# Router logits as eight more columns of the value and output projections, and a new order of TensorE's and VectorE's work in a turn

## What is computed

```python
h = concat([patches(x) @ W.T + b + pos_embed, with a class token, txt])   # 32 x 274 x 192
h = h + attention(layernorm(h))        # 12 heads of 16, rotary positions, causal, then @ Wo + bo
n = layernorm(h)                       # (h - mean) / sqrt(var + eps), no gain
pc, pu = softmax(n @ Wsc + bsc), softmax(n @ Wsu + bsu)       # 4 logits each
common = expert[argmax pc](n)          # gelu(n @ W1 + b1) @ W2 + b2
unique = expert[argmax pu](n) for tokens beyond the capacity of their common expert
out = h + common + dropped * unique
```

## Time and profile before

| | us |
|---|---|
| median of 3 runs | 1303.76 (1300.44 to 1304.24) |
| the profiled execution | 1305.39, span 1303.5 |
| PE busy in the span | 1202.0 (92%), 12718 instructions |
| DVE busy | 883.1 (68%) |
| POOL, ACT busy | 621.8 (48%), 555.9 (43%) |
| granted TensorE clock, mean | 0.962 of full |
| ACT's exponential L760, 96 of 1631 ns | 156.6 |

### The profile page before, as it was taken

One profiled execution on the slowest core, in us unless ns is written; L12 is line 12 of the kernel. 1 busy time (PEld: TensorE's weight loads), 2 busy tenths in 40 slices (PEclk: granted clock), 3 DMA queues, 4 the chain that ended last, 5 costly groups with the idle time before them and its releaser, 6 DMA issues.

```text
span 1303.5 us, 33182 instructions
## 1 busy us (share of the span) xinstructions
PE 1202.0 (92%) x12718; PEld 1026.7 (79%) x12718; DVE 883.1 (68%) x1979; ACT 555.9 (43%) x959; POOL 621.8 (48%) x990
## 2 busy tenths in 40 slices
...
DMA packets 84367, 168.03 MB, mean 129 GB/s; under 512 B 16446, under 2 KB 57701, under 8 KB 84208
## 3 DMA queue, kind: packets, MB, share of 16 engines
...
...
## 4 chain that ended last, share of the span: by engine, by line
PE 46%; DVE 22%; issue 12%; POOL 12%; DMA 3%; ACT 2%; SPq 1%; POOLq 0%; DVEq 0%; ACTq 0%
PE h_ps L1677 10%; PE y_ps L1688 9%; DVE capped L995 4%; POOL sorted_d L235 4%; PE round_banks L591 3%; PE gen L553 3%; PE gen L511 3%; POOL PT L877 3%; DVE xn L1011 3%; PE round_banks L564 3%; PE gen L520 2%; DVE nm L999 2%; DVE nm L997 2%; POOL rstd L870 2%; PE round_banks L578 2%
## 5 line engine op out<-in xcount | busy, mean ns | idle before, releaser
L760 ACT ACTIVATE PT<-round_banks 128x1752 f32<-128x1752 f32 x96 | 156.6, 1631 | 175.4 <-PE round_banks L591 175.4
L877 POOL TENSOR_SCALAR_AFFINE_SELECT PT<-PT 128x512 f32<-128x512 f32 x192 | 117.8, 637 | 206.3 <-ACT PT L760 205.8
L1767 ACT ACTIVATE Gl<-h_ps,W 128x256 f32<-128x256 f32 x264 | 115.8, 474 | 172.1 <-PE h_ps L1677 163.9
L1688 PE MATMUL y_ps<-W,Gl 128*128 128x192 f32 x1056 | 181.2, 325 | 0.0
L1688 PEld LDWEIGHTS y_ps<-W,Gl 128*128 128x128 f32 x1056 | 171.3, 189 | 0.0
L1677 PE MATMUL h_ps<-XH,Wh 128*128 128x256 f32 x528 | 149.0, 299 | 7.0 <-DVE Wl L1834 2.8
L511 PE MATMUL gen<-w_emb,xT 128*128 128x192 f32 (+1 forms) x768 | 143.8, 339 | 7.8 <-DMA ident<-in_ident_dram 7.8
L1677 PE MATMUL h_ps<-XH,Wl 128*128 128x256 f32 x528 | 141.4, 289 | 0.0
L511 PEld LDWEIGHTS gen<-w_emb,xT 128*128 128x128 f32 (+1 forms) x768 | 119.6, 171 | 16.7 <-DMA ident<-in_ident_dram 7.8
L591 PEld LDWEIGHTS round_banks<-QKT 32*128 32x128 f32 x2304 | 95.3, 187 | 46.7 <-DVE nm L997 23.0
L995 DVE TENSOR_TENSOR capped<-round_banks,masks_f 128x1024 f32<-128x1024 f32 x96 | 116.2, 1211 | 17.3 <-PE round_banks L564 16.8
...
...
## 6 DMA issues: line engine op xcount, KB each, us to landing
...
```

Source lines behind the costliest of these rows:

```text
L760: act.activation(PT[(JG * b + j) % 2][:], R[:, :, 0:438], ACT.Exp, scale=SCALE).then_inc(exps, 1)
L877: pool.affine_select(x[:, :, at:at + P], x[:, :, at:at + P], [[0, GH], [1, P]], ALU.is_ge, 0.0, base=0, channel_multiplier=-1)
L1688: mm = pe.matmul(y_ps[t.par][:, k * D:(k + 1) * D], Gl[t.par][:, f, k * P:(k + 1) * P], W[t.i][:, W2O + f * D:W2O + (f + 1) * D], start=(f ...
L1767: act.activation(Gl[t.par][:, f, :], h_ps[f % 3][:, 0:ROWS], ACT.Gelu, bias=W[t.i][:, B1O + f:B1O + f + 1]).then_inc(g_ready, 1)
```

## The change

**Logits without the second transposes.** The normed token is (h - mean) / std, and h is the residual plus attention. The router weights are centred over their 192 rows (`centre_router`), so that the mean drops out. Then `n @ Wr = (h @ Wc) / std`, and h splits in two. The part of the residual is `xn @ Wc` times the first norm's std, with `xn` already turned for the projections: V0, V1 and Vt get eight more columns of `w_qkv`. The part of attention is `att @ (Wo @ Wc)`: WO and WOt get eight more columns of `w_o`, which are mixed once, in turns 1 and 2, on PE and DVE (`turn_output_weights`, `mix_output_weights`). ACT scales the first part by std into `part` while it copies the values (a second small activation behind each); POOL makes std (`spread`); DVE adds the parts (`add_attention`); `soften` multiplies by the second norm's rstd, now kept per token in `rstd2`, and adds the bias. X2, RT, X2t and RTt, their copies, buffers and waits are gone. The second norm's scaled rows are still made and stored for the experts.

**PE's order.** The new `STEADY` stands in the diff. X and V0, QK0 move ahead of E0; E0 stands between M1 and S1 with V1; QK1 ahead of UT0; E1, AT, XTt, ATt and UTt stand between M2 and T; PV0 behind T; RK behind KQ1.

**DVE's new list**: WO add, WOt add (each behind its add of partial logits), M0, LN2 statistics, LN2t statistics, rotate QK0, LN2 scale, M1, E0 add, rotate QK1, divide UT0 and UT1, M2, E1 add, LN2t scale, T and minimum, LN1 statistics, rotate QKt, divide UTt, soften, choose, LN1 scale, position, norm of the next tail.

**The other engines.** ACT copies X ahead of the S0 weights, V1 directly behind V0, AT, XTt and ATt ahead of PV0's result. POOL takes the LN1 root behind the copy of the tail heads. SP loads `w_r` with the first constants and `r_bias` where `w_r` was. The last turns (`FINAL`) lose the same uses.

```diff
@@ -60,10 +61,9 @@
 CWIDTH = sum(CONSTS.values())
 
 
-STEADY = [("PV1", 4), ("PV2", 4), ("E0", 0), ("X", 1), ("E1", 0), ("V0", 1), ("QK0", 1), ("UT0", 4), ("UT1", 4), ("QK1", 1),
-          ("KQt0", "1"), ("KQt1", "1"), ("X2", 5), ("V1", 1), ("PV0", 3), ("XTt", "0"), ("ATt", "8"), ("RTt", "10"), ("UTt", "7"),
-          ("AT", 4), ("RT", 5), ("RK", "12"), ("QKt", "0"), ("X2t", "9"), ("KQ0", 1), ("KQ1", 1), ("MT", 2), ("Vt", "0"), ("KQ2", 1), ("WO", 4),
-          ("WOt", "8")]
+STEADY = [("PV1", 4), ("PV2", 4), ("X", 1), ("V0", 1), ("QK0", 1), ("E0", 0), ("V1", 1), ("QK1", 1), ("UT0", 4), ("UT1", 4),
+          ("KQt0", "1"), ("KQt1", "1"), ("E1", 0), ("AT", 4), ("XTt", "0"), ("ATt", "8"), ("UTt", "7"), ("PV0", 3),
+          ("QKt", "0"), ("KQ0", 1), ("KQ1", 1), ("RK", "12"), ("MT", 2), ("Vt", "0"), ("KQ2", 1), ("WO", 4), ("WOt", "8")]
 ROUNDS = [("M0", 2), ("S0", 3), ("M1", 2), ("S1", 3), ("M2", 2), ("T", 2), ("S2", 3)]
 TURNS = 4 * (NG - 1) + 12 + 1
 
@@ -71,7 +71,7 @@
 LAST = 4 * (NG - 1)
 HURRIED = {"8": LAST + 7, "9": LAST + 8, "10": LAST + 8, "11": LAST + 9, "12": LAST + 9}
 FINAL = {LAST + 7: [use for use in STEADY if use[0] not in ("ATt", "WO", "WOt")] + [("ATt", "8"), ("WO", 4), ("WOt", "8")],
-         LAST + 8: [("RK", "12"), ("X2", 5), ("X2t", "9"), ("RT", 5), ("RTt", "10")]}
+         LAST + 8: [("RK", "12")]}
 
 
 def item(lag, t):
...
@@ -261,9 +261,11 @@
         base = sb("base", [P, 2, D])
         biasb = sb("biasb", [P, 2, D])
         w_emb = sb("w_emb", [P, EC, D])
-        w_qkv = sb("w_qkv", [P, 2, 3 * D])
-        w_o = sb("w_o", [P, 2, D])
+        w_qkv = sb("w_qkv", [P, 2, 3 * D + NE])
+        w_o = sb("w_o", [P, 2, DE])
         w_r = sb("w_r", [P, 2, NE])
+        r_bias = sb("r_bias", [P, NE])
+        woT = sb("woT", [KC, 2, 2, KC + 1])
         minus_half = sb("minus_half", [P, 2])
 
...
@@ -272,6 +274,11 @@
         mv = sb("mv", [P, 4, 2, 2])
         veps = sb("veps", [P, 4, 2])
         rstd = sb("rstd", [P, 4, 2])
+        rstd2 = sb("rstd2", [P, COLS])
+        std = sb("std", [P, 2, 2])
+        stdt = sb("stdt", [P, NG])
+        part = sb("part_logits", [P, 8, 2, NE])
+        partt = sb("part_logits_t", [P, 4, NE])
         xn = sb("xn", [P, 2, D])
         xnT = sb("xnT", [KC + 1, 2, 2 * P])
...
@@ -345,9 +354,9 @@
         stage_set, pad_set = sem("stage_set"), sem("pad_set")
 
         first = ((w_emb, "w_emb"), (base, "base"), (biasb, "biasb"), (ident, "ident"))
-        loads = ((w_qkv, "w_qkv"), (cosw, "cosw"), (sinw, "sinw"), (masks, "masks"), (tmask_f, "tmask"))
-        later = ((w_o, "w_o"), (w_r, "w_r"), (K.before, "before"), (K.consts, "rconsts"))
-        n_set = 4 + 6 + 2 + 2 + 8 + 3 + 1
+        loads = ((w_qkv, "w_qkv"), (cosw, "cosw"), (sinw, "sinw"), (masks, "masks"), (tmask_f, "tmask"), (w_r, "w_r"))
+        later = ((w_o, "w_o"), (r_bias, "r_bias"), (K.before, "before"), (K.consts, "rconsts"))
+        n_set = 4 + 4 + 2 + 2 + 8 + 3 + 1
         n_late = 3
         LN1, LN2, LN1T, LN2T = range(4)
 
...
@@ -531,18 +540,36 @@
                 have("AT", b)
                 g = fill("WO", b)
                 for k in range(2):
-                    o = g[:, k * D:(k + 1) * D]
+                    o = g[:, k * DE:(k + 1) * DE]
                     pe.matmul(o, attT[:, 0, tok(k)], w_o[0:KC + 1, 0, :], start=True, stop=False)
                     mm = pe.matmul(o, attT[0:KC, 1, tok(k)], w_o[0:KC, 1, :], start=False, stop=True)
                 filled("WO", b, mm)
 
-            def route(use, i, xTs, tiles):
-                g = fill(use, i)
-                for k in range(tiles):
-                    o = g[:, k * NE:(k + 1) * NE]
-                    pe.matmul(o, xTs[:, 0, tok(k)], w_r[0:KC + 1, 0, :], start=True, stop=False)
-                    mm = pe.matmul(o, xTs[0:KC, 1, tok(k)], w_r[0:KC, 1, :], start=False, stop=True)
-                filled(use, i, mm)
+            def centre_router():
+
+                pe.wait_ge(consts_set, n_set)
+                pe.matmul(R[0:KC, 0, 0:NE], K.ones[0:KC, 0:KC], w_r[0:KC, 0, :], start=True, stop=False)
+                pe.matmul(R[0:KC, 0, 0:NE], K.ones[0:KC, 0:KC], w_r[0:KC, 1, :], start=False, stop=True).then_inc(mean_filled, 1)
+
+            def turn_output_weights():
+
+                pe.wait_ge(later_in, 16 * len(later))
+                for j in range(2):
+                    for c in range(2):
+                        at = (2 * j + c) * (KC + 1)
+                        mm = pe.transpose(R[0:KC, 1, at:at + KC + 1], w_o[0:KC + 1, c, j * KC:(j + 1) * KC], ident[0:KC + 1, 0:KC + 1])
+                mm.then_inc(wo_turned, 1)
+
+            def mix_output_weights():
+
+                pe.wait_ge(wo_copied, 1)
+                pe.wait_ge(centred, 1)
+                for c in range(2):
+                    o = R[0:KC + 1, 2, c * NE:(c + 1) * NE]
+                    pe.matmul(o, woT[:, 0, c, :], w_qkv[0:KC, 0, 3 * D:3 * D + NE], start=True, stop=False)
+                    mm = pe.matmul(o, woT[:, 1, c, :], w_qkv[0:KC, 1, 3 * D:3 * D + NE], start=False, stop=True)
+                mm.then_inc(wo_mixed, 1)
+                pe.wait_ge(wo_set, 1)
 
             def turn_heads(use, i, src, tiles, groups):
 
@@ -620,7 +647,7 @@
 
             for t in map(Turn, range(TURNS)):
                 if t.t == 2:
-                    pe.wait_ge(later_in, 16 * len(later))
+                    mix_output_weights()
                 if t.hurried and t.tail[12] is not None:
                     rank(t.tail[12])
                 if t.mid is not None:
...
@@ -752,7 +765,9 @@
 
             def copy_values(use, i, k):
                 g = take(use, i)
-                emptied(use, i, act.activation(V[i % 4][:, k, :, 0:HD], g[:, 0:D].rearrange("p (h d) -> p h d", d=HD), ACT.Copy))
+                act.activation(V[i % 4][:, k, :, 0:HD], g[:, 0:D].rearrange("p (h d) -> p h d", d=HD), ACT.Copy)
+                act.wait_ge(std_ready, i + 1)
+                emptied(use, i, act.activation(part[:, i % 8, k, :], g[:, D:DE], ACT.Copy, scale=std[:, i % 2, k:k + 1]))
 
             def weights(b, j):
 
...
@@ -867,7 +869,26 @@
                 pool.wait_ge(var_ready[which], i + 1)
                 pool.tensor_scalar(veps[:, which, 0:n], mv[:, which, 0:n, 1], EPS, None, ALU.add).then_inc(veps_ready[which], 1)
                 pool.wait_ge(veps_ready[which], i + 1)
-                pool.tensor_tensor(rstd[:, which, 0:n], veps[:, which, 0:n], minus_half[:, 0:n], ALU.pow).then_inc(rstd_ready[which], 1)
+                if which == LN2:
+                    c = UNIT * (i // 4) + 2 * (i % 4)
+                    r = rstd2[:, c:c + 2]
+                elif which == LN2T:
+                    r = rstd2[:, UNIT * i + UNIT - 1:UNIT * (i + 1)]
+                else:
+                    r = rstd[:, which, 0:n]
+                pool.tensor_tensor(r, veps[:, which, 0:n], minus_half[:, 0:n], ALU.pow).then_inc(rstd_ready[which], 1)
+
+            def spread(b):
+
+                pool.wait_ge(rstd_ready[LN1], b + 1)
+                if b >= 2:
+                    pool.wait_ge(g_emptied[bank("V1", b - 2)], nth("V1", b - 2))
+                pool.tensor_tensor(std[:, b % 2, :], veps[:, LN1, :], rstd[:, LN1, :], ALU.mult).then_inc(std_ready, 1)
+
+            def spread_tail(g):
+
+                pool.wait_ge(rstd_ready[LN1T], g + 1)
+                pool.tensor_tensor(stdt[:, g:g + 1], veps[:, LN1T, 0:1], rstd[:, LN1T, 0:1], ALU.mult).then_inc(stdt_ready, 1)
 
             def causal(b, j):
...
@@ -1047,7 +1071,14 @@
 
             def soften(u):
 
-                lg = by_token[:, cols(u), :].rearrange("p c (s e) -> p c s e", s=2)
+                dve.wait_ge(g_emptied[bank("WO", 4 * u + 3)], nth("WO", 4 * u + 3))
+                dve.wait_ge(g_emptied[bank("WOt", u)], nth("WOt", u))
+                dve.wait_ge(rstd_ready[LN2], 4 * u + 4)
+                dve.wait_ge(rstd_ready[LN2T], u + 1)
+                mine = by_token[:, cols(u), :]
+                lg = mine.rearrange("p c (s e) -> p c s e", s=2)
+                then(dve.tensor_tensor(mine, mine, bc(rstd2[:, cols(u)].rearrange("p (c a) -> p c a", a=1), [P, UNIT, NE]), ALU.mult))
+                then(dve.tensor_tensor(mine, mine, bc(r_bias[:].rearrange("p (a e) -> p a e", a=1), [P, UNIT, NE]), ALU.add))
                 then(dve.tensor_reduce(mx[:], lg, AX.X, ALU.max))
                 dve.tensor_tensor(z[:], lg, per_choice(mx[:]), ALU.subtract).then_inc(z_ready, 1)
 
...
 
+            def centre_router():
+
+                dve.wait_ge(mean_filled, 1)
+                dve.scalar_tensor_tensor(w_qkv[0:KC, :, 3 * D:3 * D + NE],
+                                         R[0:KC, 0, 0:NE].rearrange("p (a e) -> p a e", a=1).broadcast_to([KC, 2, NE]), -1.0 / D,
+                                         w_r[0:KC, :, :], ALU.mult, ALU.add).then_inc(centred, 1)
+
+            def add_attention(b):
+
+                g = take("WO", b)
+                c = UNIT * (b // 4) + 2 * (b % 4)
```

(50 more changed lines are left out.)

239 lines of the change are left out of this document (101 added, 138 removed).

## The result

| | before | after |
|---|---|---|
| median of 11 runs each, us | 1303.76 (1294.15 to 1307.99) | 1313.77 (1304.22 to 1316.53) |
| ratio, 95% interval | | 1.0075 (1.0048 to 1.0103) |
| profiled execution: time, span, mean granted clock | 1305.4, 1303.5, 0.962 | 1316.0, 1314.3, 0.941 |

The forecast was 1278.0 us with 1250 to 1298, so the direction was wrong. Over the 11 executions of the changed kernel the span follows the clock: 1302.5 us at a mean of 0.950, 1314.8 at 0.938.

What follows compares the result with a forecast made beforehand. PE's own work was taken as the bound. Steady turns 24 us, turns 2 and 3 1 us and drain 2.5, less 2 for the start, make 25.5: 1305.4 becomes 1279.9, and 1278.3 for the median; range 1250 to 1298.

Steps and rivals of the forecast that it cites:

- rival B: Waits lower the clock: the S0 wait could do that seven times, 0.9 to 1.85 us each, 1287 us; chance 0.14.
- the start: Mixing the weights at the start, transposes, copy, products, copy, each waited for: costs 2 us of 0 to 4.
- turns 32 and 33: These turns have no E0, so S1 waits longer by what X2 and RT gave: nothing gained.
- The parts that leave and come: X2 and RT leave PE, 1.29 us a turn, half that for the tail every fourth; added columns cost 0.1 a turn.
- M1 to S1: Every turn, PE waits 0.45 us for DVE, which has rotate and LN2 scales ahead of the M1 reduction; bounds 0, 0.8.
- 0.55 in the first window and 0.2 in the last: Two amounts subtracted in the sums for the first and fourth windows, which gave 23.0 and 25.05 us.
- MT at UTt's bank: In the turn with UTt, MT waits 1.0 us until DVE divides UTt behind the LN1 statistics; bounds 0 and 1.3.
- M0 to S0: Behind the turn with UTt, S0 waits 2.2 us for the tail's scale ending DVE's list; bounds 0 and 3.4.
- The windows: Four steady turns, MT to MT: 23.0, 24.65, 27.4 and 25.05 us, together 100.1 for 103.5, seven times, 24 us saved.
- The drain: RT stands on the last chain at half clock, X2 beside it; their removal saves 2.5 us of 0 to 4.
- Rival C: The DMA landing of the maxima decides S0; at 3.5 us it costs PE 50 us, 1328 us; chance 0.06.
- A: The waits don't come, DVE runs its list ahead: 1243 us, or 1260 for half of it; chance 0.20.

Runs made afterwards that it cites:

- e1: Changed kernel with the order of before in TensorE, VectorE, ScalarE and GpSimd, X2, RT and their copies left out: 1290.9 us.
- e2: Changed kernel with the scale of the next text tail's first normalization moved behind VectorE's second reduction of the next turn: 1283.1 us.
- e7: e5 with VectorE's two scales of the second normalization behind its second reduction of the turn, not ahead of it: 1258.5 us.
- e5: Changed kernel with the moves of e2 and e4, and VectorE's division of the tail's attention ahead of the LN1 statistics: 1274.6 us.
- e3: Changed kernel with five matmuls of 192 columns, result unread, ahead of X in every fourth turn, where TensorE waits before S0: 1297.7 us.
- e4: Changed kernel with the mixing of output and router weights earlier, in turn 1, its copy ahead of VectorE's scale of the tokens: 1305.2 us.
- e6: e5 with the embedding's matmuls, adds, statistics and scale in their places of before, in turns 1 and 2 alone: 1275.3 us.

## Why the prediction was wrong

The step that failed is the one in which waits cost only their length. The waits of the steady turns were forecast nearly right, but the half clock behind them stood in the sum at nothing, as rival B with 0.14; it took 13.8 us in the steady turns and about 3 more in turn 3. The second is the start, 2 us in the sum, where the stretch up to MT 4 became 13.6 us longer. The third is turns 32 and 33, "nothing" in the sum, where 3.0 us came. Each part:

- **The parts that leave and come**: nearly right. In e1 PE's busy time falls by 4.8 us in four turns; the prediction had 5.5 (1.3 a turn and 0.7 for the tails, less 0.1 a turn). Two small terms of the sum, 0.55 in the first window and 0.2 in the last, have no source in the prediction; the windows came out all the same.
- **M1 to S1**, 0.45 a turn: right on average as a wait (0.43, 0.23, 0.48 and 0.59 us in turns 21 to 24 of e2), somewhat too low as a price: taking its cause away gave 2.0 us in four turns (e7).
- **MT at UTt's bank**, 1.0: measured 1.07. As a price it was too high: with 0.8 of it gone, only 0.25 was gained (e5).
- **M0 to S0**, 2.2: measured 1.91; e2 gives 2.0 a turn back.
- **The windows**, 100.1 for four turns: 100.3 to 100.5 where the clock stayed up. Over MT 4 to MT 31 the changed kernel loses 13.8 us to half clock in turns 11, 12, 19, 23 and 27 (against e3); without it it would be 23.2 us ahead of before, for the 24 of the sum. About 2 of the 23.2 are luck: before lost them to a fall of its own in turn 14 (the windows of turns 13 and 14 are 25.30 and 26.50 us, those of turns 17 and 18 24.71 and 25.17).
- **Rival B is what happened, and was mis-sized twice.** It had 0.14 and 0.9 to 1.85 us per fall, from one window of 3.7 us. Behind S0 half clock lasted 6.8 to 10.2 us at a fall and cost 2.7 to 4.4; behind S1 of turn 13 it was 3.5 us and 1.4. The argument against it, dense work on both sides of the wait, did not hold. Before has 0.99 over its steady turns, with 0.30 us of wait at the same S0; the missing hundredth is the one fall named above. That the short waits are why there was only one is in line with e2 and e3, which have none there.
- **The start**, "2 us of 0 to 4": the size failed most plainly here. It was +7.6 to MT 2 and +6.0 to MT 4. I priced the four steps of the mixing one by one and left out what they stand behind on DVE, the scale of turn 1, itself late because E1 is late in the new order. Then came half clock from 46.0 and 69.9 us. e4 gives back 6.0 of the 7.6, e2 4.8 of the 6.0 (turn 3: 28.73 to 23.97). Some of this is the execution's luck with the clock: MT of turn 2 is at 63.9 to 65.5 us in the three kernels whose start is the same.
- **Turns 31 to 33**, "nothing": +3.0. S1 of turn 32 waits 2.44 us, since E0 was what stood there. e7, with the scales behind, waits 1.17. I had named the mechanism and given it no price.
- **The drain**, -2.5: it is -2.8 in e1 and was lost in the new order. From MT 33 to the positions of the last unit but one, behind which the last sends of the attention stage wait, there are 35.5 us before, 32.4 in e1, 36.5 after. Which move does that was not tried; e2, which leaves the drain as it is, has 34.7, so about 2 us of it can be chance. Behind it all kernels take 419.1 to 422.0 us, scatter of a part that the change doesn't touch, and +2.6 of the +3.5.
- **Rival C**, the landing: true in turn 3 alone (2.42 us), nowhere in the steady turns. **A**: e7 shows what it would have been worth, had the order been laid out for it.

The sum of the profile by cause: -23.2 in the steady turns, +13.8 half clock there, +13.6 start and turns 2 and 3, +3.0 in turns 31 and 32, +3.5 behind: +10.7, where the medians have +10. New order with old logits was not run; against e1 the new order costs 22.9 us as it was written, and with three moves on DVE and an earlier mixing (e7) it gains 32.4.

## What to carry to other kernels

Price a wait on TensorE twice: once for its length, and once for the half clock that may follow. Here the same 1.9 us cost 2 us in turns 7 and 15, and 4.7 to 6.3 in turns 11, 19, 23 and 27. Before taking work out of TensorE's order, ask which wait that work was covering; the gain is what stays when the engine that frees the buffers keeps its own pace. An in-order engine whose list ends with a wait hands that wait to the first instruction of its next turn: the place of one scale on VectorE was worth 31 us here, about three times what the columns bring by themselves (2.2% for 0.75%, e2 and e1).

## What the runs showed of the chip

- Half clock is not sure after a wait. The wait of 1.9 us was followed by it in turns 12, 20, 24 (from 609.2 us, 10.2 us long) and 28 (the others 6.8 long), not in turns 8 and 16. The profile of e4, with the same steady turns, has it in the same four.
- Shorter waits can go with it. S1 of turn 13 waits 1.4 us in six profiles; half clock followed for 3.5 us in three (changed kernel, e4, e6) and not in the other three (e2, e3, e5). In the steady turns of e2 the clock never fell.
- It came once with hardly a wait. Before has it in turn 14, the longest wait in the 6.4 us ahead being 0.37 us. PE's timeline and the windows:

```profile
359.56 0.32 PE L574 MATMUL round_banks<-tmask,identb 128*96 128x18 bf16 x4 [0.37 <-POOL QKT L927]
...
363.62 1.97 PE L591 MATMUL round_banks<-QKT 32*128 32x274 f32 x24
...
355.60:362.00 6.40, 6.03 (x96) 4.90 (x95) 6.20 (x13) 1.91 (x4) 3.69 (x6) 1.00 0.11 38
362.00:365.50 3.50, 3.50 (x33) 2.95 (x31) 0.62 (x5) 1.36 (x3) 0.00 (x0) 0.51 0.00 0
```

- TensorE's time at half clock is not all lost. 10.2 us at 1.2 GHz in turn 24 cost 4.3 us, and 6.8 us cost 2.7, where half of each would be 5.1 and 3.4. That shorter waits for other engines took up the rest is argued, not shown.
